# A place of its own for every operation of every batch in the order of a four-layer kernel's engines

## The chip, the cores and the metric

The kernel runs on one core of one Trainium2 chip. A core has TensorE (matrix products, in the profile PE, with its weight loads as PEld), VectorE (DVE), ScalarE (ACT) and GpSimd (POOL), each of which works through its own instructions in order, and SyncE (SP), which issues most transfers. The engines wait for one another by semaphores. The metric is the device time of the slowest core, here the only one, in microseconds (us).

## What is computed

A batch of 8 sequences of 128 rows with 128 channels goes through four layers. Each layer is attention and then a feed-forward network (FFN), each added to the stream with a gate, `x = x + tanh(g) * f(x_norm)`:

```python
# layer 0: 16 heads of 64 over a context, causal mask
attn = softmax(where(causal | padding, NEG, q @ k.T / sqrt(64)))     # ctx @ Wo.T
y = bitlinear(silu(bitlinear(x, w_gate)) * bitlinear(x, w_up), w_down)   # ternary weights, x rounded to 8 bits
# layer 1: 16 heads of 8 with a mask, then 8 experts, the top 2 of each row
buf = zeros.at[dest].set(xr); y = gelu(buf @ W1 + b1) @ W2 + b2; out = sum of y[dest] * gates
# layer 2: one head of 128 with padding by lengths, then a ternary FFN with gelu and a layernorm
# layer 3: 16 heads of 8 with biases, then a ternary FFN with two rmsnorms and a squared relu
```

## The kernel before

One batch fills the 128 partitions, so each stage of a layer is run once for each of the eight batches. The stages are named A0, F0 (layer 0), A1, ROUTE and MOE (layer 1, ROUTE choosing the experts and MOE running them, one expert after the other over all batches), A2, F2, A3, F3. For each engine a table `stages` holds the operations of every stage: for A0 on VectorE for instance `ln_stats` (mean and variance), `v_sb` (copies a half of the values out of a bank), `top_of` (maxima of four heads' scores), `recip0` (inverse sums of the exponentials), `ot_sb0` and `resid`.

Sixteen heads are worked in four groups of four. On TensorE `scores0` makes two groups' scores into two banks (the mask first, added as a product with the identity, line 810), ScalarE's `exps` turns them into probabilities (line 565) with VectorE's maxima, GpSimd's `norm0` multiplies them by the inverse sums (line 468), `probsT` transposes them (line 866), `probsT_sb` copies them back, `pv0` multiplies by the values, `y0` by the output weights. `proj0` makes keys, queries and values (lines 903 and 908), `xt` transposes the normalised rows (line 801), `up`, `ht` and `y_ffn` are the FFN's three products (lines 975, 986, 997). GpSimd's `rs` is the inverse root of a variance and the normalisation behind it (lines 441 to 462), `masks` makes the masks of layers 1 and 2 (lines 427 to 436), `scatter` and `fetch` move single rows to and from the experts by indirect transfers (lines 483 and 488). In A2 VectorE sums the fetched rows of a batch (`sum_stats`, line 1444), takes the maxima of its scores (`top2`, line 1270) and normalises its product (`norm2`, lines 1276 and 1278); in F3 it quantises (`quant3`, `scale3`, `square3`, `hq3`).

The order is set by pattern. `steps_of` lays the stages out in steps, with a start for each stage (`PLAN`: F0 four steps behind A0, A1 six, ROUTE eleven; then the experts; then A2, F2, A3 and F3 in the same way). In each step every stage has four slots, and in a slot each operation works on the batch that its own lag gives it; `turns` lets the stages of one slot take turns, an instruction each. So all batches have the same neighbours, apart from the first and the last ones, where stages are still or already missing. Things that are done once hang on a step's start or end: `masks` behind the second step of A0, `weight_sums` (sums of the ternary weights, which need a bank that the values had) ahead of a step, `banks_free`, `ternary_ready`, `start_inner` (waits only), `first_fetches` (the first two batches' rows) ahead of A2, where `fetch_ahead` then fetches two batches ahead.

A bank of the accumulator memory is claimed before it is written: `claim` finds which operation had it before, by the order on TensorE, and waits for the one that emptied it. So a new order gives new claims.

## Time and profile before

| | |
|---|---|
| time, median of 3 runs (lowest to highest) | 484.13 us (484.13 to 485.12) |
| span of the profiled execution | 482.6 us |
| busy in it: TensorE, its weight loads | 388.5 us (81%), 281.1 us (58%) |
| busy in it: VectorE, ScalarE, GpSimd | 287.2 us (60%), 263.1 us (55%), 180.6 us (37%) |

The profiled execution has a span of its own, 482.6 us, from its first to its last instruction; the measured times are 1.5 us and more above it, for what lies around. The span is read here by stages: A0 and F0 up to some 150, A1 and ROUTE up to some 260, the experts up to 305, A2 and F2 up to some 360, A3 and F3 to the end. A row of the timeline has the start, the duration, the engine, the line and the operation, the tiles, and in brackets how long the engine stood idle before it and which instruction ended that. A row of the table by windows has for each engine the busy time in the stretch and the granted clock of TensorE (PEclk; 1.00 is 2.4 GHz, 0.50 is 1.2 GHz).

### The profile page before, as it was taken

How to read it: one execution, taken by the hardware profiler on the slowest of the kernel's cores; microseconds unless marked ns; L12 is line 12 of the kernel's file. 1: busy time of each engine (PE TensorE's matmuls, PEld its weight loads, DVE VectorE, ACT ScalarE, POOL GpSimd, SP SyncE). 2: the span in 40 equal slices, each digit the busy share in tenths (PEclk: the TensorE clock that was granted, in tenths of full speed). 3: DMA queues.
4: the chain of work that ended last, by engine and by line, in shares of the span. 5: the costliest groups of instructions: out<-in, count | busy, mean ns of one | idle time of the engine just before them, and what ended most of it. 6: DMA issues, size and time to landing. Idle time of an engine off the chain costs nothing.

```text
span 482.6 us, 9945 instructions
## 1 busy us (share of the span) xinstructions
PE 388.5 (81%) x3550; PEld 281.1 (58%) x3564; DVE 287.2 (60%) x859; ACT 263.1 (55%) x781; POOL 180.6 (37%) x294
## 2 busy tenths in 40 slices
PE   3866999999997898999962999427778999889633
PEld 0645777767876665665541899315555666665522
DVE  3151575688687878665562121643546566898884
ACT  3234757676675778877631433422464766555532
POOL 3186334333424311355363000388726442221120
PEclk9597999999999999999985899855699999999955
DMA  8990000000000030000003241111000000000001
GB/s 338 394 381 6 1 2 1 1 2 2 2 1 1 1 133 1 1 13 18 20 22 93 59 130 36 45 33 27 7 0 1 3 1 1 2 2 3 3 0 43
DMA packets 7135, 22.11 MB, mean 46 GB/s; under 512 B 1215, under 2 KB 3503, under 8 KB 6575
## 3 DMA queue, kind: packets, MB, share of 16 engines
q1 hardware_dynamic: 6063, 19.38, 11.1%
q0 software_dynamic: 1024, 2.10, 1.5%
q8 instruction: 29, 0.48, 0.4%
q14 instruction: 19, 0.16, 0.1%
HBM read 14.60 MB, written 6.88 MB: 44 GB/s over the span
## 4 chain that ended last, share of the span: by engine, by line
PE 61%; ACT 11%; POOL 9%; DVE 7%; issue 7%; DMA 3%; SPq 0%; POOLq 0%; another core or an unknown queue 0%; DVEq 0%; ACTq 0%
PE bank L839 6%; PE bank L908 6%; PE bank L866 5%; ACT prob L565 5%; PE bank L1031 4%; PE bank L1022 3%; POOL moe_rows L488 3%; PE bank L822 3%; PE bank L854 3%; PE bank L903 3%; PE bank L917 3%; PE bank L810 3%; DVE mx L1236 3%; PE bank L888 2%; PE bank L975 2%
## 5 line engine op out<-in xcount | busy, mean ns | idle before, releaser
L565 ACT ACTIVATE prob<-bank,mx 128x128 f32<-128x128 f32 x256 | 82.3, 384 | 23.4 <-DVE mx L1236 23.2
L1236 DVE TENSOR_REDUCE mx<-bank 128x4 f32<-128x512 f32 x96 | 63.9, 682 | 41.0 <-PE bank L839 21.5
L468 POOL TENSOR_TENSOR prob<-prob,rden 128x512 f32<-128x512 f32 x32 | 33.2, 1039 | 69.2 <-DVE rden L1258 69.2
L550 ACT ACTIVATE probT<-bank 128x512 f32<-128x512 f32 x64 | 39.5, 617 | 29.9 <-PE bank L866 29.8
L866 PE MATMUL bank<-pack,prob 128*128 128x128 f32 x256 | 41.5, 286 | 7.6 <-POOL prob L468 4.6
L443 POOL TENSOR_TENSOR rstd<-rstd,minus_half 128x1 f32<-128x1 f32 x72 | 41.3, 573 | 6.0
L441 POOL TENSOR_SCALAR rstd<-mv 128x1 f32<-128x1 f32 x64 | 12.4, 193 | 83.0 <-DVE mv L1211 79.6
L866 PEld LDWEIGHTS bank<-pack,prob 128*128 128x128 f32 x256 | 28.7, 143 | 16.4 <-POOL prob L468 6.6
L488 POOL DMA_INDIRECT moe_rows<-yrows_d,row_of x16 | 16.0, 999 | 52.2 <-DMA yrows_d<-o_n 48.3
L462 POOL TENSOR_SCALAR xn<-pack,mv,rstd 128x128 f32<-128x128 f32 x32 | 25.9, 811 | 5.9 <-POOL rstd L443 5.4
L565 ACT ACTIVATION_READ_ACCUMULATOR prob<-bank,mx 128x1 f32 x128 | 27.9, 218 | 0.0
L888 PE MATMUL bank<-probT,vz 128*32 128x128 f32 x512 | 26.9, 282 | 0.6 <-ACT probT L583 0.6
L839 PE MATMUL bank<-kz,qz 64*128 64x512 f32 x96 | 26.4, 626 | 0.5 <-issue 0.5
L583 ACT ACTIVATE probT<-bank 128x512 f32<-128x512 f32 x32 | 18.1, 594 | 14.7 <-PE bank L854 14.6
L891 PE MATMUL bank<-probT,pack 128*32 128x128 f32 x512 | 25.7, 273 | 0.0
L550 ACT ACTIVATE xnT<-bank 128x128 f32<-128x128 f32 x40 | 11.3, 282 | 25.6 <-PE bank L801 25.5
L1247 DVE COPY va<-bank 128x512 f32<-128x512 f32 x16 | 11.0, 688 | 21.4 <-PE bank L903 21.4
L908 PE MATMUL bank<-xnT,pack 128*128 128x128 f32 x128 | 20.6, 311 | 3.1 <-ACT xnT L550 2.9
L810 PE MATMUL bank<-neg,identb 128*128 128x512 bf16 x64 | 20.4, 381 | 3.2 <-ACT prob L565 3.1
L908 PE MATMUL bank<-pack 128*128 128x128 f32 x128 | 18.5, 290 | 4.7 <-DMA pack<-pack_d 2.8
L1435 DVE TENSOR_TENSOR o_n<-bank,pack 90x256 f32<-90x256 f32 (+1 forms) x16 | 4.9, 349 | 28.7 <-PE bank L1031 28.7
L908 PEld LDWEIGHTS bank<-xnT,pack 128*128 128x128 f32 x128 | 18.4, 219 | 6.0 <-ACT xnT L550 4.6
(233 smaller groups left out, 965.2 us busy)
## 6 DMA issues: line engine op xcount, KB each, us to landing
yrows_d<-moe_rows SPq DMA_DIRECT2D x2, 1510.0 KB, 21.2
pack<-pack_d SPq DMA_DIRECT2D x1, 2112.0 KB, 15.7
expert<-experts_d SPq DMA_DIRECT2D x4, 514.0 KB, 8.5
pack<-experts_d SPq DMA_DIRECT2D x4, 514.0 KB, 5.1
pack<-pack_d SPq DMA_DIRECT2D x1, 2048.0 KB, 10.3
xrows_d<-moe_rows SPq DMA_DIRECT2D x1, 1080.0 KB, 21.0
moe_rows<-xrows_d SPq DMA_DIRECT2D x8, 135.0 KB, 3.0
yrows_d<-o_n SPq DMA_DIRECT2D x8, 135.0 KB, 1.8
```

Source lines behind the costliest of these rows:

```text
L443: pool.tensor_tensor(out, out, minus_half, ALU.pow).then_inc(ev.sem, 1)
L462: pool.tensor_scalar(out, x_sb[:, it.b, :], mv[layer][:, k, 0:1], rstd[layer][:, k, 0:1], ALU.subtract, ALU.mult).then_inc(ev.sem, 1)
L468: pool.tensor_tensor(part, part, r.to_broadcast([P, GH, P]), ALU.mult).then_inc(E[A0]["norm"].sem, 1)
L488: pool.indirect_dma_start(y_got[:, b, j, :], None, yrows_d, bass.IndirectOffsetOnAxis(ap=row_of[:, b, j:j + 1], axis=0)).then_inc(y_fetche ...
L550: act.activation(dst, src, ACT.Identity if kw else ACT.Copy, **kw).then_inc(E[layer][name].sem, 1)
L565: act.activation(prob[:, g % 2, P * j:P * j + P], bank[S_BANK[g % 2]][:, P * j:P * j + P], ACT.Exp, bias=mx[:, g % 2, j:j + 1], **kw).then ...
L810: pe.matmul(bank[S_BANK[g % 2]][:, :].rearrange("p (h t) -> p h t", h=GH), identb[:, :], (neg0 if layer == A0 else neg1)[:, bass.ds(it.b, ...
L839: pe.matmul(bank[S_BANK[a]][:, :].rearrange("p (h t) -> p h t", h=GH), qz[rows, it.k, c, :], kt[c if layer == A3 else 0][rows, it.b, :, :] ...
L866: mm_ = pe.transpose(bank[T_BANK[g % 2]][:, P * j:P * j + P], prob[:, g % 2, P * j:P * j + P], ident)
L888: pe.matmul(out[QW * j:QW * j + QW, 0:P], vz[:, it.k, QW * h:QW * h + QW], probT[:, g, P * j:P * j + P], start=(g == 0), stop=(g == G - 1) ...
L908: mm_ = pe.matmul(out[:, P * t:P * t + P].rearrange("p (a n) -> p a n", a=1), w[:, 512 * c + P * t:512 * c + P * t + P], rhs, start=True, ...
L1236: dve.tensor_reduce(out, bank[S_BANK[g % 2]][:, :].rearrange("p (h t) -> p h t", h=GH), AX.X, ALU.max, negate=True).then_inc(E[layer]["max ...
```

## The change

`walk` no longer goes through steps. Every entry of `stages` has eight numbers, a place for each batch, and each engine does its operations in the order of these numbers. An operation of several instructions (a generator) goes back into the queue after each of them with its place raised by `TURN`, so that two such operations can alternate. The things done once have a place too. `steps_of`, `turns`, `LAG` and `PLAN` are gone; the waits that hung on a step's start are now at the operation that needs them, and VectorE has some waits that the fixed pattern had made unnecessary. The instructions of each engine are the same ones.

```diff
+def walk(stages, once=(), run=lambda layer, fn, it, *args: fn(it, *args)):
+    queue = []
+    for layer, entries in stages.items():
+        for b in range(B):
+            for fn, *args, places in entries:
+                if places[b] is not None:
+                    queue.append((places[b], len(queue), run, (layer, fn, Item(b, b), *args)))
+    for at, fn in once:
+        queue.append((at, len(queue), fn, ()))
+    while queue:
+        at, n, begin, args = head = min(queue, key=lambda entry: entry[0:2])
+        queue.remove(head)
+        rest = begin(*args)
+        if rest is not None:
+            if next(rest, stages) is not stages:
+                queue.append((at + TURN, n, lambda rest=rest: rest, ()))
...
-PLAN = (steps_of({F0: 4, A0: 0, A1: 6, ROUTE: 11})
-        + [("steps", [(MOE, s)]) for s in range(NE + 2)]
-        + steps_of({A2: 0, F2: 3, A3: 8, F3: 13}))
+TURN = 0.203
...
+        E[A0]["mean"] = Event(wsum_dve, 0, len(TERNARY))
+        emptied[A0, "w"] = ("mean", 1)
...
-                    [(3, rs, A2), (2, fetch_ahead)],
+                    (fetch_ahead, (322.8, 334.816, 338.348, 287.3, 310.874, 347.278, 324.985, 338.972)),
+                    (rs, A2, (308.589, 313.824, 338.456, 339.08, 343.782, 344.785, 351.472, 352.962))],
...
+            walk(stages, [(-7.2, masks), (279.7, first_fetches)])
...
                 found = before_in_bank(layer, piece, it.rep)
                 if found is None:
+                    if bank_of(layer, piece, it.rep) in K4_BANK[0]:
+                        pe.wait_ge(k4_act, 4)
+                        pe.wait_ge(k4_dve, 4)
                     return
...
             def up(it, layer, piece, w, lhs):
                 wait(pe, layer, "xt_sb", it)
+                if it.rep == 0 and layer == F0:
+                    pe.wait_ge(tern_dve, 9)
+                if it.rep == 0 and layer == F2:
+                    pe.wait_ge(k4_act, 12)
+                    pe.wait_ge(k4_dve, 12)
...
-            def weight_sums():
+            def weight_sums(it):
                 pe.wait_ge(wsum_dve, len(TERNARY))
-                wait(pe, A0, "v_sb", Item(2, 2))
+                claim(it, A0, "w")
                 pe.matmul(bank[R_BANK[0]][:, 0:len(TERNARY)], ones, asum[:, :], start=True, stop=True).then_inc(wsum_pe, 1)
-                pe.wait_ge(wsum_dve, len(TERNARY) + 1)
...
+                wait(dve, layer, "rs", it.back(2))
```

Three places in the order follow, before and after.

The first is VectorE at the start, from the copies of batch 0's last four pieces of keys (`kz`) on. `BN_STATS` and `BN_AGGR` are a batch's statistics, `va` the values, `mx` the maxima of the scores. Before:

```order
L1532 TENSOR_SCALAR kz<-bank,pack 128x4x128 x4
L1210 BN_STATS stats<-pack 128x6
L1211 BN_AGGR mv<-stats 128x2
L1247 COPY va<-bank 128x512 x2
L1210 BN_STATS stats<-pack 128x6
L1211 BN_AGGR mv<-stats 128x2
L1236 TENSOR_REDUCE mx<-bank 128x4 x2
```

After:

```order
L1508 TENSOR_SCALAR kz<-bank,pack 128x4x128 x4
L1183 BN_STATS stats<-pack 128x6
L1184 BN_AGGR mv<-stats 128x2
L1220 COPY va<-bank 128x512
L1183 BN_STATS stats<-pack 128x6
L1184 BN_AGGR mv<-stats 128x2
L1220 COPY va<-bank 128x512
L1209 TENSOR_REDUCE mx<-bank 128x4 x2
```

The statistics of batch 1 stand between the two copies instead of behind both.

The second is TensorE from the last maxima of layer 0 to the first of layer 1: `neg,identb` with `k,qT` is half of a batch's scores, here of batch 7, `prob` the transposes, `probT,va` the product with the values, `oT` the output, `hid` and `t_downT` the FFN. Before:

```order
L810 MATMUL bank<-neg,identb 128x512 x2
L822 MATMUL bank<-k,qT 128x128 x8
L866 MATMUL bank<-pack,prob 128x128 x4
L876 MATMUL bank<-probT,va 64x128 x8
L810 MATMUL bank<-neg,identb 128x512 x2
L822 MATMUL bank<-k,qT 128x128 x8
L866 MATMUL bank<-pack,prob 128x128 x4
```

After:

```order
L754 MATMUL bank<-neg,identb 128x512 x2
L766 MATMUL bank<-k,qT 128x128 x8
L820 MATMUL bank<-probT,va 64x128 x8
L810 MATMUL bank<-pack,prob 128x128 x8
L861 MATMUL bank<-pack,oT 128x128 x8
L939 MATMUL bank<-pack,hid 128x128 x4
L950 MATMUL bank<-t_downT,hqT 128x128 x4
L754 MATMUL bank<-neg,identb 128x512 x2
L766 MATMUL bank<-k,qT 128x128 x8
```

Between the two halves of the scores stand four more of the transposes, an output product and the two products of an FFN.

The third is where A2 begins, on GpSimd (`moe_rows` is a gather, two for each batch; the three rows behind it an inverse root and its normalisation), and on VectorE (`moe_rows` the sums, two for each batch, `mx` the maximum, `rden` and `o_n` the normalisation). GpSimd before:

```order
L488 DMA moe_rows<-yrows_d,row_of 128x128 x6
L441 TENSOR_SCALAR rstd<-mv 128x1
L443 TENSOR_TENSOR rstd<-rstd,minus_half 128x1
L462 TENSOR_SCALAR pack<-pack,mv,rstd 128x128
L488 DMA moe_rows<-yrows_d,row_of 128x128 x2
L441 TENSOR_SCALAR rstd<-mv 128x1
L443 TENSOR_TENSOR rstd<-rstd,minus_half 128x1
L462 TENSOR_SCALAR pack<-pack,mv,rstd 128x128
L488 DMA moe_rows<-yrows_d,row_of 128x128 x2
```

After:

```order
L438 DMA moe_rows<-yrows_d,row_of 128x128 x6
L391 TENSOR_SCALAR rstd<-mv 128x1
L393 TENSOR_TENSOR rstd<-rstd,minus_half 128x1
L412 TENSOR_SCALAR pack<-pack,mv,rstd 128x128
L438 DMA moe_rows<-yrows_d,row_of 128x128 x2
L391 TENSOR_SCALAR rstd<-mv 128x1
L393 TENSOR_TENSOR rstd<-rstd,minus_half 128x1
L412 TENSOR_SCALAR pack<-pack,mv,rstd 128x128
L438 DMA moe_rows<-yrows_d,row_of 128x128 x6
```

By the table the first six gathers are those of batches 0, 1 and 2 before and of 0, 1 and 5 after, and the last six of after are those of 2, 3 and 4. VectorE before, from the second batch's sums on:

```order
L1444 SCALAR_TENSOR_TENSOR pack<-moe_rows,w_tok,pack 128x128 x2
L1210 BN_STATS stats<-pack 128x6
L1211 BN_AGGR mv<-stats 128x2
L1270 TENSOR_REDUCE mx<-bank 128x1
L1444 SCALAR_TENSOR_TENSOR pack<-moe_rows,w_tok,pack 128x128 x2
L1210 BN_STATS stats<-pack 128x6
L1211 BN_AGGR mv<-stats 128x2
L1270 TENSOR_REDUCE mx<-bank 128x1
L1276 RECIPROCAL rden<-rden 128x1
```

After:

```order
L1243 TENSOR_REDUCE mx<-bank 128x1
L1420 SCALAR_TENSOR_TENSOR pack<-moe_rows,w_tok,pack 128x128 x2
L1183 BN_STATS stats<-pack 128x6
L1184 BN_AGGR mv<-stats 128x2
L1420 SCALAR_TENSOR_TENSOR pack<-moe_rows,w_tok,pack 128x128 x2
L1183 BN_STATS stats<-pack 128x6
L1184 BN_AGGR mv<-stats 128x2
L1249 RECIPROCAL rden<-rden 128x1
L1251 TENSOR_SCALAR o_n<-bank,rden 128x128
L1243 TENSOR_REDUCE mx<-bank 128x1
```

Behind the first batch's maximum stand the sums of two batches, 2 and 3, instead of one, and then batch 0's normalisation ahead of batch 1's maximum.

## Rows read from the trace of the kernel before

**Rows 1.** The page's first lines: span, and busy time of each engine.

```profile
span 482.6 us, 9945 instructions
...
PE 388.5 (81%) x3550; PEld 281.1 (58%) x3564; DVE 287.2 (60%) x859; ACT 263.1 (55%) x781; POOL 180.6 (37%) x294
```

**Rows 2.** Windows: stretch and length, each engine's busy time, PEclk, DMA.

```profile
41.00:138.00 97.00, 91.59 (x809) 71.75 (x811) 65.06 (x183) 65.06 (x254) 36.26 (x49) 0.98 0.01 2
138.00:160.00 22.00, 18.80 (x178) 15.01 (x179) 16.04 (x46) 15.51 (x62) 8.74 (x11) 1.00 0.01 1
160.00:248.00 88.00, 82.01 (x922) 52.05 (x922) 61.62 (x192) 65.41 (x209) 34.49 (x58) 1.00 0.08 26
...
305.00:346.00 41.00, 21.74 (x82) 13.40 (x80) 21.13 (x73) 14.00 (x39) 30.94 (x46) 0.58 0.11 29
346.00:367.00 21.00, 15.05 (x83) 10.78 (x83) 10.62 (x37) 13.38 (x29) 9.94 (x21) 0.92 0.00 1
367.00:447.00 80.00, 74.91 (x908) 51.07 (x914) 60.57 (x173) 48.10 (x97) 25.70 (x57) 1.00 0.01 2
```

**Rows 3.** Timeline of VectorE at the start: start, duration, operation, idle before.

```profile
24.53 0.69 DVE L1247 COPY va<-bank 128x512 f32<-128x512 f32 x1 [2.08 <-PE bank L903]
```

**Rows 4.** Timeline of GpSimd at the start.

```profile
25.72 0.19 POOL L441 TENSOR_SCALAR rstd<-mv 128x1 f32<-128x1 f32 x1 [11.06 <-DVE mv L1211]
...
32.23 6.21 POOL L436 TENSOR_SCALAR neg<-pack,lens_f,qneg 128x128 bf16<-128x128 f32 x8
38.41 2.03 POOL L468 TENSOR_TENSOR prob<-prob,rden 128x512 f32<-128x512 f32 x2
```

**Rows 5.** Timeline of TensorE at the start.

```profile
19.81 1.92 PE L903 MATMUL bank<-pack 128*128 128x512 f32 x2
...
39.49 1.11 PE L866 MATMUL bank<-pack,prob 128*128 128x128 f32 x4 [4.37 <-POOL prob L468]
```

**Rows 6.** Windows: the stretch of the low clock near 40.

```profile
37.40:44.20 6.80, 4.71 (x18) 3.98 (x19) 0.18 (x1) 3.48 (x14) 4.08 (x5) 0.50 0.00 0
```

**Rows 7.** Timeline of SyncE's queue: issue of the large mask's load.

```profile
3.90 0.45 SPq L379 DMA_DIRECT2D mask_i<-mask_d  x1
```

**Rows 8.** The tile of that mask: time from issue to landing.

```profile
DMA to landing us min/median/max: 16.4/16.4/16.4
```

**Rows 9.** Timeline of TensorE at the last scores of layer 0.

```profile
149.56 0.39 PE L810 MATMUL bank<-neg,identb 128*128 128x512 bf16 x1 [0.71 <-ACT prob L565]
151.44 0.39 PE L810 MATMUL bank<-neg,identb 128*128 128x512 bf16 x1 [1.50 <-ACT prob L565]
```

**Rows 10.** Timeline of GpSimd behind the experts: first gather, first root, next gather.

```profile
307.87 0.99 POOL L488 DMA_INDIRECT moe_rows<-yrows_d,row_of  x1 [48.29 <-DMA yrows_d<-o_n]
...
315.29 0.19 POOL L441 TENSOR_SCALAR rstd<-mv 128x1 f32<-128x1 f32 x1
...
317.22 1.08 POOL L488 DMA_INDIRECT moe_rows<-yrows_d,row_of  x1 [0.18 <-issue]
```

**Rows 11.** Timeline of VectorE there: batch 1's maximum.

```profile
323.13 0.29 DVE L1270 TENSOR_REDUCE mx<-bank 128x1 f32<-128x128 f32 x1 [2.78 <-PE bank L957]
```

**Rows 12.** Transfers issued from 305 to 335: count, median us to landing.

```profile
moe_rows<-yrows_d,row_of POOLq DMA_INDIRECT x15, 2.5
```

**Rows 13.** Timeline of TensorE: second down projection of F2, first scores of A3.

```profile
359.60 0.49 PE L994 MATMUL bank<-crow,pack 128*128 128x128 f32 x2 [1.74 <-ACT hid L550]
...
367.44 1.13 PE L839 MATMUL bank<-kz,qz 64*128 64x512 f32 x4 [0.48 <-issue]
```

**Rows 14.** Timeline of TensorE at the tail: batch 7's output product.

```profile
462.05 0.79 PE L942 MATMUL bank<-pack 128*128 128x128 f32 x2 [5.09 <-DVE pack L1226]
```

**Rows 15.** Timeline of VectorE at the tail: batch 7's normalisation, batch 3's last residual.

```profile
457.81 0.94 DVE L1263 RECIPROCAL rsum<-bank 128x128 f32<-128x128 f32 x1
...
458.78 0.29 DVE L1265 TENSOR_TENSOR oT<-bank,rsum 128x128 f32<-128x128 f32 x1
...
461.66 0.34 DVE L1226 SCALAR_TENSOR_TENSOR pack<-bank,hs,pack 128x128 f32<-128x128 f32 x1
```

426 lines of the change are left out of this document (205 added, 221 removed).

## The prediction

> **What bounds the kernel now.** Read first the busy shares: TensorE is busy 388.5 of 482.6 us, VectorE 287.2, ScalarE 263.1 [rows 1]. An average hides where time can be won, so next the table by stage [rows 2]. In the three attention stretches with sixteen heads TensorE stands still little: 97.00 - 91.59 = 5.4 us in 41 to 138, 88.00 - 82.01 = 6.0 in 160 to 248, 80.00 - 74.91 = 5.1 in 367 to 447. The larger holes are between: about half of 305 to 346 is idle and the granted clock there is 0.58 of full, 346 to 367 has 6.0 us idle, 138 to 160 has 3.2 us. A new order can win only at these seams, at the start, at the tail, or by closing the 16.5 us of small gaps in the dense stretches.
>
> The change keeps every operation and its tile; it only gives each a new neighbour on its engine, and moves some waits from a step's head to the operation that needs them. So no instruction is added or taken away, and each term below is a wait that goes, shrinks or appears. I followed each engine's new order by hand through the rows' times.
>
> **The start: minus 4.0 us.** On VectorE the statistics of batch 1 stand behind both copies of batch 0's values. The second copy starts at 24.53, after a wait of 2.08 us for TensorE, and takes 0.69 [rows 3]; the statistics follow it. GpSimd, which waits 11.06 us for them, then does batch 1's inverse root at 25.72, the twelve mask instructions up to 32.23 + 6.21 = 38.4, and only then the first normalisation, at 38.41 [rows 4]. TensorE's first transposes of probabilities wait 4.37 us for that [rows 5]. While it waits its clock falls: 37.4 to 44.2 has 4.71 us of matmul at 0.50 [rows 6].
>
> In the new order TensorE does batch 0's first values ahead of its first queries, and VectorE takes batch 1's statistics between the two copies. The values, 1.92 us from 19.81 on [rows 5], then start in the queries' place, behind the transposed rows near 17.6; they need only the context, which is there, and the copy is at about 19.6 to 20.3, the statistics end near 20.9, and GpSimd's row of 25.72 moves to about 21.0. The large mask was asked for at 3.90 us [rows 7] and took 16.4 us to land [rows 8], so it was there at 20.3 and holds nothing up. It is then through its masks at 33.7 and the first normalisation moves by 4.7 us. TensorE has more to do before that point (the second values of batch 1 are put ahead of the transposes), so its wait nearly goes, and with it the low clock: 4.71 us at half speed are 2.35 at full. The ceiling is therefore 4.37 + 2.35 = 6.7, the floor 0 if TensorE were the later one all the same. Following the rows on, the last of batch 0's four transposes comes 3.9 us earlier and the scores of batch 2 stay ahead by 3.75. I take 4.0, near the normalisation's own 4.7, less a little for the new order's extra work ahead.
>
> **First to second attention: minus 1.5 us.** At 149.56 and 151.44 TensorE waits 0.71 and 1.50 us, because the last scores of batch 7 need banks that ScalarE's exponentials must empty, and those wait for a maximum that stands behind the gated FFN's quantisation on VectorE [rows 9]. The new order puts batch 6's first product with the values, two transposes, batch 5's output and batch 3's down projection between the two halves of the scores, some 5 us of ready work. Bounds 0 and 2.2; I take 1.5, since the work drawn forward leaves small holes behind it.
>
> The Trainium skill (Perfetto Trace Analysis, Optimization Strategy) says that a kernel whose most contended engine changes over time may gain by interleaving those regimes. By that rule all the idle time of 138 to 160, 22.00 - 18.80 = 3.2 us, could go, and the sum below would be -7.7 and the time 476.4. The rows show only 2.2 us of it at the place that the new order touches, so I stay with 1.5.
>
> **The gathers of the third attention: plus 0.5 us, bounds -2 and +6.8.** Here the new order looks worse. After the experts GpSimd gathers two sets of rows for each batch; three batches take 315.29 - 307.87 = 7.42 us, 2.47 each, and an inverse root holds the next gather up by 317.22 - 315.29 = 1.93 [rows 10]. Before, it gathers 0, 1 and 2, and then alternates one inverse root and one gather. After, it gathers 0, 1, 5, then 6, and only then 2, 3 and 4, all three in a row. And VectorE now has the sums of batches 2 and 3 ahead of batch 0's normalisation and batch 1's maximum. So that maximum, which comes at 323.13 [rows 11], must wait for batch 3's rows: GpSimd reaches the gather of 3 at 307.87 + 5 x 2.47 + 2 x 1.93 = 324.1, ends it at 326.5, the rows land 2.5 us after their issue [rows 12], about 1.5 after its end, and two sums, the statistics and the normalisation take 1.9 us. That is 329.9, or +6.8. Batch 0's residual comes 4.6 us later by the same reckoning.
>
> What catches it: batches 2 to 4 then come close together, where before each pair of gather and root, 2.47 + 1.93 = 4.4 us, set their distance, and the third FFN's second transpose now stands ahead of the first down projection, so that TensorE's wait of 1.74 us at 359.60 shrinks [rows 13]. By hand the first up projection comes 4 us later, the second down projection 1.5 us later than 359.60, and the scores of the fourth attention at 367.44 are at -1 to +0.5 [rows 13]. I take +0.5. The upper bound is open to one more thing, the clock: TensorE has 15.05 us of matmul in 346 to 367 at 0.92 [rows 2], and if it stayed at 0.50 there, these would take 0.92 / 0.50 - 1 = 0.84 times as long again, 12.6 us, part of it in idle gaps. The forecast counts nothing for it; the second rival does.
>
> **The tail: minus 1.0 us.** Batch 7's output product waits 5.09 us, to 462.05 [rows 14]. Its normalised rows are ready at 458.78 + 0.29 = 459.07, but its bank is emptied by batch 3's last residual, at 461.66, behind 2.6 us of quantisation on VectorE [rows 15]. The new order puts that residual ahead of the normalisation. The output could come 462.05 - 459.07 = 3.0 us earlier; behind it VectorE has a full row of quantisations that are as many as before. Bounds 0 and 3.0; I take 1.0. Route and experts: no seam moves by more than 0.3 us, nothing.
>
> **The dense stretches: 0, bounds -2 and +2.** Each pass of a batch is set by the loop scores, maximum, exponential, transposes, and its members are all still there. Some exponentials now stand back to back, which saves a wait; a few outputs now follow their last product at once, with the normalisation between them exposed (from 457.81 to 459.07 it takes 1.26 us [rows 15]; one or two such places are the 2 us of either bound). These cancel as far as I can follow them. The weight sum of the ternary layers has a place of its own, and the mean on VectorE follows it there without TensorE waiting for it: nothing.
>
> **Sum.** -4.0 - 1.5 + 0 + 0.5 - 1.0 = -6.0 us on the profiled execution's span, 482.6 to 476.6. The median of 484.13 lies 1.5 us above that span, and nothing at either end of the program changes, so 478.1 is the time.
>
> **Rivals.** (1) *No change.* The third attention's 6.8 us pass on in full and cancel the -6.5 of the other terms: 484.4. For it: TensorE is idle for half of that stage, and behind a late batch 1 there is not much other work. Against: the chain there is one of several, and batches 2 to 4 catch up.
>
> (2) *Slower.* The same one mechanism, the gathers of 5 and 6 ahead of 2 and 3, with the clock: TensorE, idle longer, stays at half clock up to the fourth attention. To the 6.8 us come 0.84 x 15.05 = 12.6, of which I let a third be felt where the matmuls stand in the chain, 4.2: -6.5 + 6.8 + 4.2 = +4.5, 488.6. It decides as soon as the first up projection comes over 5 us late and the stretch 346 to 367 shows a clock under 0.7. For it: the clock was 0.58 over 305 to 346 [rows 2], and it comes back only when TensorE works more closely. Against: the FFN's matmuls come closer together in the new order.
>
> (3) *Much faster.* The dense stretches tighten too. They hold 5.4 + 6.0 + 5.1 = 16.5 us of TensorE's idle time; half of it and the forecast's 6.0 give 469.9, all but a sixth of it 464. For it: with a place for each operation an order can fit each batch, where one pattern before served all eight. Against: my walk along the rows found no place where many of these gaps go; ScalarE and VectorE are each busy 65.06 of the 97.00 us [rows 2] and stand in the same loop. The Trainium skill (Perfetto Trace Analysis, Identifying the Most-Contended Engine) says that matmul busy time is a bad measure of how near the roofline is, and weight-load busy time a better one; weight loads fill 71.75 of 97.00 us in 41 to 138 [rows 2], 74%, so by it more than the idle time could go.
>
> (4) *It does not do what it says:* an operation stands behind a wait that a later one on another engine must release, or a claim of a bank is late everywhere, and the kernel slows by tens of us. I see no such place.
>
> **Chances.** Forecast (475.5 to 482) 0.42; no change 0.13; slower 0.19; much faster 0.24; the rest 0.02, slower. The range leaves out a tenth on each side: from the middle of the much faster case, 468.5, to the slower case's price, 489. About 0.2%, 1 us, is what a measurement of this kernel can tell from no change. Of the no-change case 0.11 lies within that and 0.01 on either side. Faster by more: 0.42 + 0.24 + 0.01 = 0.67; same 0.11; slower 0.19 + 0.02 + 0.01 = 0.22.
>
> **What would show it.** Start: GpSimd's first normalisation near 33.7 instead of 38.4, and no stretch at half clock around 40. First to second attention: under 1 us of waits for exponentials around 146 to 150. Third attention: batch 1's maximum 6 us later against the end of the experts, the fourth attention's first scores within 1 us of before, both counted from the end of the experts. Tail: no 5 us wait for the bank of the output. The forecast is wrong if the dense stretches change length by over 2 us each, or if the third attention's delay reaches the fourth.

## The result

The changed kernel takes 509.09 us (median of 4 runs, 508.50 to 509.18) against 484.13 us (483.57 to 485.12), a ratio of 1.0512 with an interval of 1.0492 to 1.0532. It is slower by 25.0 us where the forecast was 6.0 us faster, and 20.1 us above the upper end of the range.

The first lines of the page of after, to be read beside [rows 1]:

```profile
span 507.3 us, 10007 instructions
PE 387.7 (76%) x3550; PEld 279.3 (55%) x3564; DVE 287.6 (57%) x859; ACT 261.6 (52%) x781; POOL 182.3 (36%) x294
```

The counts by engine are those of before and the busy times lie within 2 us of it (the 62 instructions more are none that count as busy); the span is 24.7 us longer. So nothing costs more: all of the loss is time in which engines stand still.

Where it lies is told by the windows of after, cut about where the program's places answer to the windows of [rows 2], with the start (13 to 41 before) ahead of them (stretch and length, busy time of TensorE, weight loads, VectorE, ScalarE, GpSimd, granted clock, DMA):

```profile
13.00:40.00 27.00, 22.73 (x124) 15.88 (x124) 6.73 (x16) 9.01 (x33) 16.50 (x23) 0.94 0.87 333
35.00:145.00 110.00, 93.32 (x830) 72.97 (x833) 66.22 (x184) 65.40 (x255) 39.71 (x52) 1.00 0.02 7
145.00:172.00 27.00, 20.78 (x195) 15.77 (x195) 17.91 (x55) 16.18 (x65) 9.33 (x14) 1.00 0.01 1
172.00:269.00 97.00, 78.28 (x842) 48.96 (x846) 60.96 (x184) 63.61 (x204) 32.72 (x55) 1.00 0.07 24
388.00:474.00 86.00, 75.57 (x935) 53.36 (x938) 61.91 (x176) 46.57 (x93) 25.48 (x56) 0.98 0.01 2
```

The second to the fourth line are layers 0 and 1. TensorE is busy 93.32 + 20.78 + 78.28 = 192.4 us in them, and in [rows 2] 91.59 + 18.80 + 82.01 = 192.4: nearly the same work (1867 products for 1909, since the windows do not cut at the same ones). But it is idle 41.6 us of 234 there, where it was idle 14.6 us of 207. The granted clock is 1.00, so no clock explains it. The last line, layer 3, has 10.4 us idle for 5.1.

One length says the same in one number, and can be read off every run: from the start of the first product with the values of batch 0 to the start of the last product with the routing's weights. It is 205.6 us before and 233.6 us after, 28.0 more. The start ahead of it is 3.4 us shorter (46.05 for 49.47), and what follows it up to the end of TensorE's last product (224.1 us before, 224.3 after) is as long as it was. I call this length the **front**, and what follows it the **back**. The windows that cut there, before and then after:

```profile
49.47:255.05 205.58, 187.22 (x1864) 134.76 (x1872) 143.99 (x430) 140.68 (x504) 81.61 (x120) 0.99 0.04 13
46.05:279.61 233.56, 190.09 (x1865) 134.99 (x1872) 145.54 (x432) 140.94 (x502) 80.54 (x117) 0.99 0.03 12
```

With the same products but one, TensorE is idle 18.4 us before and 43.5 after: 25.1 of the 28.0 us are idle time.

These lengths come from one execution of each kernel, and the start is not the same in every one: in the five traces whose start has the order of before (before, e1, e3, e5, e6), the first product with the values is at 48.3 to 50.5; in the four with that of after (after, e2, e4, e11) it is at 45.5 to 46.2. A difference of 1 or 2 us between the starts of two traces can be chance.

What TensorE waits for there, totals of the waits by line in 35 to 269 of after (us in total, times, longest):

```profile
PE bank L754 <- ACT prob L498: 11.5, 14, 2.0
PE bank L870 <- ACT xnT L483: 3.0, 3, 1.2
PE bank L847 <- DVE va L1220: 2.1, 1, 2.1
PE bank L810 <- ACT prob L498: 2.0, 3, 0.9
```

The same view of before, 41 to 248:

```profile
PE bank L810 <- ACT prob L565: 3.1, 5, 1.5
PE bank L801 <- ACT k L550: 2.3, 6, 0.4
PE bank L908 <- ACT xnT L550: 2.2, 6, 0.4
```

Before, TensorE has many waits of 0.4 us. After, one line leads: the mask ahead of a batch's scores (`mask_scores`, L754) waits 14 times, up to 2.0 us, for a bank that ScalarE's exponentials (`exps`, L498) have to empty; 13 times it is the second of the two banks. It is 8.4 us more than the same line had before (L810, 3.1 us), so it is not the whole loss. Summed over all lines of the two views, the waits grow from 13.4 to 40.3 us: those that ScalarE ends from 10.8 to 30.7, those that VectorE ends from 2.1 to 7.4, GpSimd's from 0.2 to 1.7. The rest of ScalarE's share is copies, one or a few times each.

One of these waits, first on TensorE of after (start, duration, line, operation, idle before and what ended it):

```profile
99.88 1.06 PE L852 MATMUL bank<-pack 128*128 128x128 f32 x8
100.78 0.38 PE L754 MATMUL bank<-neg,identb 128*128 128x512 bf16 x1
102.98 0.39 PE L754 MATMUL bank<-neg,identb 128*128 128x512 bf16 x1 [1.83 <-ACT prob L498]
```

And on ScalarE of after:

```profile
99.05 0.37 ACT L498 ACTIVATE prob<-bank,mx 128x128 f32<-128x128 f32 x1 [2.27 <-DVE mx L1209]
...
100.44 1.09 ACT L483 ACTIVATE probT<-bank 128x512 f32<-128x512 f32 x2
101.39 0.40 ACT L498 ACTIVATE prob<-bank,mx 128x128 f32<-128x128 f32 x1
...
102.42 0.42 ACT L498 ACTIVATE prob<-bank,mx 128x128 f32<-128x128 f32 x1
102.76 0.65 ACT L483 ACTIVATE k<-bank 128x512 f32<-128x512 f32 x1
```

ScalarE does two groups of four exponentials, about 1.4 us each, with two copies of transposed probabilities between them. The second group ends at 102.84, and TensorE, which has the mask of the first bank done and wants the second, stands from 101.15 to 102.98. The keys that TensorE made at 99.88 are copied behind all that, from 102.76. The first group had itself waited 2.27 us for VectorE's maxima.

The same pass before, on TensorE:

```profile
97.74 1.09 PE L876 MATMUL bank<-probT,va 128*64 128x128 f32 x16
99.22 0.30 PE L801 MATMUL bank<-pack,xn 128*128 128x128 f32 x1 [0.39 <-ACT k L550]
99.89 1.16 PE L908 MATMUL bank<-xnT,pack 128*128 128x128 f32 x8 [0.37 <-ACT xnT L550]
100.89 1.02 PE L903 MATMUL bank<-pack 128*128 128x512 f32 x2
101.75 0.59 PE L810 MATMUL bank<-neg,identb 128*128 128x512 bf16 x2
```

And on ScalarE:

```profile
98.13 0.38 ACT L565 ACTIVATE prob<-bank,mx 128x128 f32<-128x128 f32 x1
...
98.47 0.61 ACT L550 ACTIVATE k<-bank 128x512 f32<-128x512 f32 x1
98.95 0.62 ACT L550 ACTIVATE probT<-bank 128x512 f32<-128x512 f32 x1
99.56 0.28 ACT L550 ACTIVATE xnT<-bank 128x128 f32<-128x128 f32 x1
99.74 0.36 ACT L565 ACTIVATE prob<-bank,mx 128x128 f32<-128x128 f32 x1
```

Here too three copies stand between the two groups. But each is one that TensorE needs at once: it is released twice after 0.4 us (99.22, 99.89), and with products, a transpose, queries and values to do, it comes to the mask only when both groups are through, so the mask has no wait at all.

### The profile page after: what moved, and what is told of

The parts are those of the page before. It is cut to its first block and busy times, and to the rows that moved or that the text cites. A ratio compares the mean times of both kernels' runs of the same rounds, so it can differ in the third digit from the quotient of the medians.

```text
span 507.3 us, 10007 instructions
## 1 busy us (share of the span) xinstructions
PE 387.7 (76%) x3550; PEld 279.3 (55%) x3564; DVE 287.6 (57%) x859; ACT 261.6 (52%) x781; POOL 182.3 (36%) x294
## 3 DMA queue, kind: packets, MB, share of 16 engines
q1 hardware_dynamic: 6063, 19.38, 10.4%
## 5 line engine op out<-in xcount | busy, mean ns | idle before, releaser
L498 ACT ACTIVATE prob<-bank,mx 128x128 f32<-128x128 f32 x256 | 81.7, 387 | 17.7 <-DVE mx L1209 13.3
L483 ACT ACTIVATE probT<-bank 128x512 f32<-128x512 f32 x64 | 37.9, 610 | 25.2 <-PE bank L810 25.0
L810 PE MATMUL bank<-pack,prob 128*128 128x128 f32 x256 | 39.0, 280 | 7.8 <-ACT prob L498 2.0
L810 PEld LDWEIGHTS bank<-pack,prob 128*128 128x128 f32 x256 | 28.1, 141 | 16.6 <-issue 6.9
L754 PE MATMUL bank<-neg,identb 128*128 128x512 bf16 x64 | 22.3, 394 | 11.7 <-ACT prob L498 11.5
L498 ACT ACTIVATION_READ_ACCUMULATOR prob<-bank,mx 128x1 f32 x128 | 29.0, 226 | 0.0
L783 PE MATMUL bank<-kz,qz 64*128 64x512 f32 x96 | 27.7, 653 | 1.0 <-ACT qz L483 0.8
L516 ACT ACTIVATE probT<-bank 128x512 f32<-128x512 f32 x32 | 18.5, 596 | 13.0 <-PE bank L798 12.9
L433 POOL DMA_INDIRECT xrows_d<-xn_all,row_of x16 | 16.5, 1029 | 23.4 <-DVE row_of L1383 20.8
L847 PE MATMUL bank<-pack 128*128 128x512 f32 x32 | 19.9, 707 | 5.1 <-DVE va L1220 2.1
L483 ACT ACTIVATE k<-bank 128x512 f32<-128x512 f32 x16 | 9.8, 612 | 22.4 <-PE bank L852 22.4
## 6 DMA issues: line engine op xcount, KB each, us to landing
pack<-pack_d SPq DMA_DIRECT2D x1, 2048.0 KB, 10.4
```

The lines of the kernel that those rows point to most:

```text
L483: act.activation(dst, src, ACT.Identity if kw else ACT.Copy, **kw).then_inc(E[layer][name].sem, 1)
L498: act.activation(prob[:, g % 2, P * j:P * j + P], bank[S_BANK[g % 2]][:, P * j:P * j + P], ACT.Exp, bias=mx[:, g % 2, j:j + 1], **kw).then ...
L754: pe.matmul(bank[S_BANK[g % 2]][:, :].rearrange("p (h t) -> p h t", h=GH), identb[:, :], (neg0 if layer == A0 else neg1)[:, bass.ds(it.b, ...
L783: pe.matmul(bank[S_BANK[a]][:, :].rearrange("p (h t) -> p h t", h=GH), qz[rows, it.k, c, :], kt[c if layer == A3 else 0][rows, it.b, :, :] ...
L810: mm_ = pe.transpose(bank[T_BANK[g % 2]][:, P * j:P * j + P], prob[:, g % 2, P * j:P * j + P], ident)
L847: mm_ = pe.matmul(out[:, :], ctxT[:, it.b, :], col["wvT_0"][:, 512 * c:512 * c + 512], start=True, stop=True)
```

## The experiments

Four theories were put to the test. **P** (theory A in the expectations of e1 to e3): some places of the table are bad in the front, and it is the order there, not the new waits. **A1** (not the stage of that name): ScalarE's places keep a ready operation waiting. **S**: ScalarE's groups of exponentials stand ahead of copies that TensorE needs next. **T**: TensorE's own order leaves too little between an operation and the one that needs its result, and no order of the other engines mends that; V in the expectations is the contrary. Other letters are explained in the expectation that uses them.

The runs in one table: the measured median and that of before measured beside it, the ratio with its interval, and the lengths of front and back from the trace, which is one execution.

| run | us | before | ratio | front, back |
|---|---|---|---|---|
| before | | 484.13 | | 205.6, 224.1 |
| after | 509.09 | 484.13 | 1.0512 [1.0492, 1.0532] | 233.6, 224.3 |
| e1_front_pattern | 483.24 | 485.25 | 0.9973 [0.9947, 1.0000] | 205.2, 222.9 |
| e2_back_pattern | 509.74 | 485.25 | 1.0512 [1.0459, 1.0565] | 234.9, 224.7 |
| e3_all_pattern | 485.34 | 485.25 | 1.0006 [0.9988, 1.0024] | 205.2, 224.0 |
| e4_start_only | 482.25 | 485.0 | 0.9945 [0.9927, 0.9963] | 206.3, 224.6 |
| e5_third_only | 481.08 | 485.0 | 0.9922 [0.9891, 0.9953] | 205.2, 221.4 |
| e6_tail_only | 481.64 | 485.0 | 0.9938 [0.9910, 0.9967] | 205.2, 222.9 |
| e7_act_by_ready | 510.7 | 485.0 | 1.0530 [1.0502, 1.0559] | 238.3, 223.8 |
| e8_after_short_exp | 491.51 | 484.29 | 1.0134 [1.0107, 1.0161] | 216.1, 223.9 |
| e9_before_short_exp | 476.32 | 484.29 | 0.9824 [0.9797, 0.9850] | 198.6, 223.9 |
| e10_copies_first | 507.72 | 484.29 | 1.0473 [1.0446, 1.0501] | 229.8, 223.0 |
| e11_three_edges | 476.48 | 484.29 | 0.9830 [0.9804, 0.9856] | 206.6, 218.9 |
| e12_after_by_ready | 516.46 | 485.2 | 1.0645 [1.0621, 1.0669] | 242.2, 224.3 |
| e13_before_by_ready | 511.31 | 485.2 | 1.0565 [1.0524, 1.0606] | 232.0, 224.2 |
| e14_after_act_need | 500.43 | 484.42 | 1.0345 [1.0303, 1.0388] | 225.2, 222.0 |
| e15_before_act_need | 494.24 | 484.42 | 1.0196 [1.0166, 1.0226] | 215.9, 224.0 |
| e16_before_act_ready | 501.36 | 484.42 | 1.0335 [1.0295, 1.0374] | 223.4, 223.5 |

### Which half, and order or waits: e1, e2, e3

The old walk by steps stands beside the new one, and each engine takes one or the other for the front half (layers 0 and 1 and the experts) and the back half; the waits are those of after in all three. In these lines the letters S and T are not the theories: S is the pattern by steps, T the tables.

```diff
+BY = {'pe': 'ST', 'act': 'ST', 'dve': 'ST', 'pool': 'ST'}    # e1_front_pattern
+BY = {'pe': 'TS', 'act': 'TS', 'dve': 'TS', 'pool': 'TS'}    # e2_back_pattern
+BY = {'pe': 'SS', 'act': 'SS', 'dve': 'SS', 'pool': 'SS'}    # e3_all_pattern
...
+        if BY[name][half] == "S":
+            walk_steps(None, plans[half], {n: old[n] for n in old if n in halves[half]}, before, after, run)
+        else:
+            walk({n: stages[n] for n in stages if n in halves[half]}, [(at, fn) for h, at, fn in once if h == half], run)
```

> The changed kernel, but up to the end of the experts every engine has the order of the kernel before; from the third attention on the tables stay. Theory A (the tables of the first two layers cost the time: TensorE stands idle there 24 us more, the stages behind them are worth nothing either way, +24.4 us at the third attention's first product and +24.7 at the end): 484 to 485 us. Theory B (the new waits, which this kernel keeps, cost a good part): 490 to 505. Theory C (the loss of the second half is only hidden because the first half is late): 488 or more.

> The other way round: tables up to the end of the experts, the order of the kernel before from the third attention on. Theory A: 508 to 510 us. Theory C: 503 or less. By the trace the third attention gains 3 to 6 us by its table and the fourth gives them back, so that this kernel should have the third attention later and the fourth shorter than the changed kernel, with the same end.

> The order of the kernel before on every engine and for all stages, with the waits of the changed kernel where it has them (at the first use of a bank, at the operation that needs a weight, and the extra ones on VectorE). Theory A: 484.1 us within 1. Theory B: 490 to 505, since only the waits differ from the kernel before.

With the old order in the front the kernel is at 483.24, with the old order in the back at 509.74. So the loss is all in the order of the first two layers and the experts. The back's order is worth 2 us at most: e1 is 2.1 us below e3, at the edge of what the intervals tell apart, and e2 and after have the same ratio. With the old order everywhere and the new waits kept it is at 485.34, a ratio of 1.0006 [0.9988, 1.0024]: the waits that were moved cost nothing that shows. P stands, for the half; which engine's places, these runs don't say.

### The prediction's three terms, each alone: e4, e5, e6

The old order, written as positions, with the order of after in one place only: the first 44.5 us, the third attention up to the first scores of the fourth, the last 33 us. Of each a line or two:

```diff
-                    (rs, A0, (0, 1, 7, 12, 17, 23, 29, 35)),
+                    (rs, A0, (0, 1, 5, 8, 17, 23, 29, 35)),            # e4_start_only
-                    (proj0, 'v', 0, (4, 12, 26, 43, 59, 78, 99, 120)),
+                    (proj0, 'v', 0, (3, 11, 26, 43, 59, 78, 99, 120)), # e4_start_only
-                    (fetch_ahead, (74, 76, 78, 80, 82, 84, 99999, 99999)),
+                    (fetch_ahead, (78, 79, 80, 74, 76, 85, 99999, 99999)), # e5_third_only
-                    (resid, A3, (592, 616, 643, 672, 701, 728, 750, 771))],
+                    (resid, A3, (592, 616, 643, 672, 701, 734, 743, 771))], # e6_tail_only
```

> The order of the kernel before on every engine, but for the operations that the changed kernel begins in its first 44.5 us: those stand in front in the changed kernel's order. The forecast's term of the start alone. Theory A (the start's 4 us are real, and it is the later passes' order that spends them): the scores of batch 2 come some 4 us earlier than before and the lead stays to the end, 480 to 481.5 us. Rival D (the lead is lost to whatever comes next, in any order): 484 to 485.

> The order of the kernel before, but for the third attention and what the changed kernel begins up to the fourth attention's first scores: those stand in the changed kernel's order, the gathers of batches 5 and 6 ahead of 2 and 3 among them. Theory E (the delay of batch 1's maximum is more than made good by the batches that follow closely): the fourth attention's first scores 3 us or more earlier than before, 480 to 482 us. Rival (the delay passes on, as the slower case of the forecast had it): 486 or more.

> The order of the kernel before, but for what the changed kernel begins in its last 33 us, which stands behind the rest in the changed kernel's order: the forecast's term of the tail alone. By the traces the changed kernel's last 33 us win 1 to 3 us against the kernel before: 481.5 to 483.5 us. Rival (the residual ahead of the normalisation only moves VectorE's work): 484 to 486.

All three are faster, by 2.8, 3.9 and 3.4 us against before measured beside them, and by 2.0, 2.0 and 1.0 us of span in the one execution traced. e5 and e6 came out as expected; e4 lies between the 481.5 of its theory and the 484 of the rival.

The start gives about what was worked out and keeps most of it: against the trace of before TensorE is 3.3 us ahead at the first product with the values and 4.07 us at the last scores of layer 0. There it meets the two waits of [rows 9] unchanged, and it loses 1.5 us on the way into layer 1; 2.0 us are left at the end. TensorE of e4:

```profile
145.49 0.39 PE L754 MATMUL bank<-neg,identb 128*128 128x512 bf16 x1 [0.71 <-ACT prob L498]
147.37 0.39 PE L754 MATMUL bank<-neg,identb 128*128 128x512 bf16 x1 [1.50 <-ACT prob L498]
```

In the third attention batch 1's maximum is as late as worked out, but the first scores of the fourth attention come earlier. VectorE, then TensorE, of e5 (the first gather starts at 308.69, 0.82 later than in [rows 10]):

```profile
330.50 0.28 DVE L1243 TENSOR_REDUCE mx<-bank 128x1 f32<-128x128 f32 x1
```

```profile
363.78 1.13 PE L783 MATMUL bank<-kz,qz 64*128 64x512 f32 x4
```

Against [rows 11] the maximum is 7.4 us later, 6.5 counted from the gathers; against [rows 13] the scores are 3.7 us earlier, 4.5 counted so. At the tail of e6 the wait for the bank is gone, and a shorter one for the normalised rows is in its place:

```profile
461.69 0.80 PE L895 MATMUL bank<-pack,oT 128*128 128x128 f32 x2 [3.08 <-DVE oT L1238]
```

### ScalarE by readiness, and exponentials made short: e7, e8, e9, e10

In e7 each operation of ScalarE up to the routing has the moment as its place at which its inputs were there in the trace of after; in e10 the same, with the groups of exponentials put back by up to 1.2 us. A line of each, of batch 0 to 7:

```diff
-                    (exps, A0, 2, (39.34, 57.487, 70.625, 86.716, 108.646, 127.366, 135.779, 151.197)),
-                    (probsT_sb, A0, 1, (39.706, 54.248, 74.486, 93.26, 107.316, 123.836, 139.751, 153.799)),
+                    (exps, A0, 2, (-22.405, -9.17, 9.256, 28.1, 47.9, 67.552, 86.327, 102.984)),           # e7_act_by_ready
+                    (exps, A0, 2, (-21.873, -7.97, 10.456, 28.483, 49.1, 68.752, 86.362, 103.673)),        # e10_copies_first
+                    (probsT_sb, A0, 1, (-21.075, -8.733, 14.986, 28.615, 48.337, 68.551, 90.452, 103.849)), # e7 and e10
```

In e8 (after) and e9 (before) the four exponentials of a group are one instruction. These two kernels leave out the maxima of a group's other three heads in the exponent and the sums of their exponentials:

```diff
             def exps(it, layer, g):
...
+                if it.rep >= 1 or layer == A1:
+                    kw = dict(accum_out=den0[:, g % 2, 0:1]) if layer == A0 else {}
+                    act.activation(prob[:, g % 2, :], bank[S_BANK[g % 2]][:, :], ACT.Exp,
+                                   bias=mx[:, g % 2, 0:1], **kw).then_inc(E[layer]["probs"].sem, GH)
+                    return
```

> The changed kernel, but ScalarE's places up to the end of the routing are new: its operations stand in the order in which, in the changed kernel's trace, their inputs were ready. All other engines stay as changed. Theory A1 (ScalarE's own order, which keeps copies waiting behind operations that are not ready or long, makes TensorE wait): a third or more of the 24 us comes back, 492 to 501 us. Rival A2 (the places of TensorE and VectorE are as much to blame, and ScalarE only passes on their lateness): 505 to 510.

> The changed kernel with shorter exponentials in the first two attentions: from the second batch on (in the second attention from the first) each group of four heads is one ScalarE instruction over 512 columns with the first head's maximum, instead of four over 128 columns, so that ScalarE holds its queue 0.6 us where it held it 1.4; the other heads' maxima are left out of the exponent and their sums are not taken. All orders stay. Theory S (what TensorE waits for in the changed kernel is mostly a copy or an exponential that stands ready while ScalarE is at another one, 22 of 38 us by the trace, against 6 of 15 before): 12 us or more come back, 497 us or less, and the distance to the kernel before with the same shorter exponentials falls from 25 to 15 us or less. Rival O (the order is to blame by what it makes wait for what, ScalarE's time is not): both kernels gain alike and the distance stays above 20.

> The kernel before with the same shorter exponentials (the same parts left out). Theory S: it has little to gain, 0 to 6 us, 478 to 485 us. Rival O: as much as the changed kernel.

> The changed kernel, but ScalarE's places up to the end of the routing are new: by the time at which the inputs were ready in the changed kernel's trace, as in the experiment before, but exponentials of the first two attentions are put back by up to 1.2 us, never past the point at which they began, so that a copy that comes within that time goes first. Theory S: better than by readiness alone (510.7), 500 to 508 us, since a copy that TensorE waits for no longer stands behind a whole group of exponentials that came just before it; not near 484, since the exponentials themselves are waited for too. Rival O: 509 to 513.

e7 felled A1 as far as readiness goes. Worked out from the semaphores in the traces, over the 224 operations that ScalarE has up to the routing, the mean time from inputs ready to start is 0.54 us before, 0.96 after and 0.55 in e7: e7 nearly halves the wait of after and yet stays at 510.7. A mean says nothing on which operation waits. The pattern of before lets the gate's tanh wait (0.94 us) and layer 0's exponentials (0.92), and the small copies that TensorE needs next hardly at all: 0.07 us for the FFN's rounded rows (`xq_sb`), 0.15 for layer 1's transposed rows (`xt_sb`), 0.18 for layer 0's queries. In e7 the gate waits 0.05 and the exponentials 0.74, but these copies 1.15, 0.80 and 0.74; in after they waited 1.06, 0.79 and 0.60.

That led to S. The one instruction takes 0.69 us where the four took 1.4. ScalarE of e9:

```profile
95.19 0.69 ACT L565 ACTIVATE prob<-bank,mx 128x512 f32<-128x512 f32 x1 [1.70 <-DVE mx L1241]
```

With it after gains 17.6 us and before 8.0, so the distance falls from 24.8 to 15.2 us. Some 10 us of the loss therefore hang on how long a group of exponentials takes. S is half right: before gained more than the 0 to 6 us of S, so it too waits for the exponentials. And the two runs don't tell a group that keeps other work from ScalarE from a group whose own result comes too late: the shorter one helps both. e10, the cheap cure by S, is at 507.72, inside S's 500 to 508 at its very edge; that is 3 us better than e7 and 1 to 2 us better than after, no more.

### The same rule on both kernels: e12, e13, e16, and e14, e15

In e12 (after) and e13 (before) TensorE keeps its order, and ScalarE, VectorE and GpSimd each do their operations in the order in which the inputs were there in that kernel's trace. In e16 (before) only ScalarE does so: e7 is its counterpart. In e14 (after) and e15 (before) ScalarE goes by the latest start at which nothing in that kernel's trace would come later. A line or two of each, in positions (the lines that go are the orders of before and, last, of after, in the same form):

```diff
-                    (xt_sb, A0, (2, 8, 21, 34, 47, 62, 78, 94)),
-                    (exps, A0, 2, (12, 25, 38, 52, 68, 84, 100, 113)),
-                    (probsT_sb, A0, 1, (14, 27, 40, 54, 70, 86, 102, 114)),
+                    (xt_sb, A0, (2, 9, 22, 35, 48, 63, 79, 95)),            # e13, e16
+                    (exps, A0, 2, (12, 25, 38, 52, 67, 83, 99, 112)),       # e13, e16
+                    (probsT_sb, A0, 1, (14, 27, 40, 55, 71, 87, 103, 115)), # e13, e16
+                    (xt_sb, A0, (2, 7, 18, 31, 44, 59, 75, 91)),            # e15
+                    (exps, A0, 2, (11, 25, 37, 52, 68, 84, 100, 113)),      # e15
...
-                    (probsT_sb, A0, 1, (13, 26, 41, 54, 69, 84, 103, 114)),
+                    (probsT_sb, A0, 1, (14, 25, 41, 52, 68, 84, 103, 114)), # e12
+                    (probsT_sb, A0, 1, (14, 29, 42, 53, 71, 87, 101, 115)), # e14
```

> The changed kernel with TensorE's order as it is, but up to the end of the routing ScalarE, VectorE and GpSimd take their operations in the order in which the inputs were ready in the changed kernel's trace (operations of one kind keep their order among themselves, and VectorE's operations of several instructions stand by their beginning). Theory T (TensorE's order sets when work comes to the other engines, in bunches, and no order of theirs mends that): 503 to 512 us. Theory V (VectorE's or GpSimd's own order costs what ScalarE's did not): 498 us or less.

> The same with the kernel before: its TensorE order, and up to the end of the routing the three other engines by the readiness in its own trace. Theory T: the order of the other engines matters little while TensorE's stays, 483 to 488 us, so that this kernel and the one above, which have the same rule for three engines, differ by 18 us or more. Theory V: 490 us or more, since the pattern of the other engines was what made it good.

> The changed kernel, but up to the end of the routing ScalarE takes its operations in the order of the latest moment at which each could begin without anything in the changed kernel's trace coming later (by need, not by readiness). Theory V (the table's ScalarE order does not fit what TensorE needs next): 8 us or more come back, 501 us or less. Theory T (TensorE's order is at fault, whatever ScalarE does): 505 to 512.

> The kernel before with the same rule for ScalarE, by need in its own trace: the control for the rule. If an order by need is a good one, 482 to 487 us; if it is 495 or more, the rule itself is bad and the experiment with the changed kernel says nothing of theory T.

> The kernel before with ScalarE by readiness in its own trace, the other engines as they were. With all three helpers by readiness it took 511.3 us. If ScalarE's order is what cost that (copies behind exponentials that were ready a little earlier): 500 us or more. If VectorE's or GpSimd's: 490 or less.

e13 is the run that settled most, against T: with TensorE's good order untouched, the helpers' order alone costs 26 us, as much as the whole change. And e16 shows that ScalarE alone brings 17 of these. Yet in e16 no operation of ScalarE is moved by more than two positions; 104 of the 224 are moved. The waits of TensorE in e16, 35 to 270:

```profile
PE bank L745 <- ACT k L483: 7.3, 6, 2.1
PE bank L852 <- ACT xnT L483: 5.4, 6, 1.2
```

In before the same two waits were 2.3 and 2.2 us, also six times each. The copy of a batch's second half of the keys stood behind the rest of a group of exponentials before too, 0.65 us in most batches; now more of the group is ahead of it, and it waits 0.99 to 2.36 us. That of the transposed rows never waited and now waits 0.77 us in five batches. The mean wait on ScalarE is 0.42 us in e16, lower than before. ScalarE and then TensorE of e16, where the keys were ready at 105.60:

```profile
105.23 0.36 ACT L498 ACTIVATE prob<-bank,mx 128x128 f32<-128x128 f32 x1
...
106.60 0.61 ACT L483 ACTIVATE k<-bank 128x512 f32<-128x512 f32 x1
```

```profile
107.36 0.30 PE L745 MATMUL bank<-pack,xn 128*128 128x128 f32 x1 [0.74 <-ACT k L483]
```

In e13 the two waits are as long (7.2 and 5.4 us), and one that GpSimd ends comes on top, for the normalised probabilities (`norm0`):

```profile
PE bank L810 <- POOL prob L418: 9.8, 8, 2.1
```

What they stand behind, on GpSimd or on VectorE, was not followed.

With ScalarE by the same rule the two kernels stand at 510.7 and 501.36 (readiness, by ratios 1.0530 and 1.0335) and at 500.43 and 494.24 (need): 6 to 9 us apart, not 25. (The runs of e14 lie 495.34 to 502.76, so its distance is the less certain.) With all three helpers by readiness they are 5.2 us apart (e12, e13) where T asked for 18 or more; e12 itself, at 516.46, is slower than either theory had it, so the rule makes after worse as well. e14 is the one order tried for after that helps clearly, by 8 to 9 us; its waits, 35 to 260, show the leading line shorter and spread:

```profile
PE bank L754 <- ACT prob L498: 6.8, 11, 0.9
PE bank L810 <- POOL prob L418: 4.0, 6, 1.8
```

e15 warns of reading too much into it: the rule itself costs before 9.8 us, and its 494.24 lies just under the 495 from which, by its expectation, e14 says nothing of T.

**What is shown and what stays open.** Shown: the loss is order, not waits (e3); it is in the front (e1, e2); an order of the three helpers alone can cost as much (e13), and one of ScalarE alone two thirds of it (e16); with one rule for ScalarE in both kernels, 16 to 19 of the 25 us between them go. That ScalarE's table carries that much of the change is likely and not shown: the rules slow before by 10 to 26 us, and may cover what the other tables cost. By the front's length of the traces the rest is larger, 9 to 15 of 28 us. Open: how the loss is shared among the tables of the four engines. A kernel with one engine's table from after and the others from before would tell; it wasn't run.

### The three edges together: e11

> The order of the kernel before, with the changed kernel's order in three places at once: its first 44.5 us, the third attention up to the fourth attention's first scores, and the last 33 us. By the traces of the three apart they win 2.4, 2.2 and 1.2 us. Theory A (the edges are independent): 5 to 8 us less than the kernel before, 477 to 479 us where the latter has 484 to 485. Rival D: less than 3 us.

The edits are those of e4, e5 and e6 in one kernel. It takes 476.48 us, 0.9830 [0.9804, 0.9856] of before, and beats both kernels. The start is 3.7 us shorter, the front 1.0 longer, the back 5.2 shorter: together the 7.8 us of its span's gain (474.8 for 482.6). By the medians it gains 7.8 us too, within the 5 to 8 of its theory and less than the 10.0 that the three have in sum. What the third attention does for it shows in the window from the experts' end to the fourth attention's first scores, which lasts 62.8 us before. Before, then e11:

```profile
304.60:367.40 62.80, 37.19 (x165) 24.34 (x164) 32.36 (x110) 27.77 (x68) 41.20 (x67) 0.70 0.07 19
302.00:359.50 57.50, 32.52 (x156) 21.76 (x155) 32.31 (x108) 27.40 (x68) 40.43 (x65) 0.73 0.08 21
```

The stretch is 5.3 us shorter, with 9 of 165 products put behind it and the clock at 0.73 for 0.70. TensorE's idle time in it hardly changes, 25.0 us for 25.6.

## Why the prediction was wrong

**The dense stretches, "0, bounds -2 and +2", are the step that failed.** The front, which holds two of the three and the seam between them, became 28.0 us longer, and the third, layer 3, some 5 us. "Its members are all still there" was true and beside the point: the loop of scores, maximum, exponential and transposes was kept, but what stands between its members on ScalarE wasn't followed: of the 26.9 us that TensorE's waits grew by in the dense part, ScalarE ends 19.9. How far its own table is to blame stays open, as said above. "Some exponentials now stand back to back, which saves a wait" is neither borne out nor the fault: up to the routing two groups stand next to each other at 1 place of ScalarE's order before and at 12 in after, but also at 15 in e14, which is faster than after, and at 4 in e7, which is not. The walk along the rows covered the start, three seams and the tail, and no pass in the middle, where the pattern repeats and where all of the loss is. A term that repeats in every pass can't be bounded by "one or two such places": the one wait at L754 alone came 14 times and to 11.5 us, for 5 times and 3.1 us before. In layer 3 it is VectorE that TensorE waits for: the view of 387.1 to 483.6 of after, and that of 367.4 to 456.1 of before:

```profile
PE bank L789 <- DVE mx L1209: 5.3, 5, 2.4
```

```profile
PE bank L845 <- DVE mx L1236: 1.8, 3, 0.8
```

**The start, -4.0, was right in mechanism and measured 3.4.** The second half of batch 0's values no longer holds the statistics up. VectorE and GpSimd of after:

```profile
21.04 0.69 DVE L1220 COPY va<-bank 128x512 f32<-128x512 f32 x1 [8.23 <-PE bank L847]
21.65 0.28 DVE L1183 BATCH_NORM_STATS2 stats<-pack 128x6 f32<-128x128 f32 x1
```

```profile
28.74 6.21 POOL L386 TENSOR_SCALAR neg<-pack,lens_f,qneg 128x128 bf16<-128x128 f32 x8
34.92 1.03 POOL L418 TENSOR_TENSOR prob<-prob,rden 128x512 f32<-128x512 f32 x1
```

The first normalisation is at 34.92, 3.5 earlier than in [rows 4] and 1.2 later than worked out, since the copy came at 21.04 and not at 20. TensorE's wait of 4.37 [rows 5] is gone, with waits of 1.66 us (31.77) and 1.98 (42.72) in its place, and the clock over the start is 0.94 where it was 0.75 before:

```profile
13.00:41.00 28.00, 18.75 (x105) 13.94 (x104) 7.55 (x15) 7.77 (x26) 15.62 (x20) 0.75 0.84 321
```

The size is good to about 2 us, by the spread of the start between traces; the means of the five traces and the four above are 3.5 us apart. The gain was there at the first product with the values and was spent by the next passes; e4 keeps most of it.

**First to second attention, -1.5, did not come.** Work was drawn forward between the two halves of batch 7's scores, but the masks still wait: 0.71 us at the first half (153.21) and 1.16 at the second, 1.9 in sum where [rows 9] has 2.2. On TensorE of after:

```profile
160.56 0.39 PE L754 MATMUL bank<-neg,identb 128*128 128x512 bf16 x1 [1.16 <-ACT prob L498]
```

And the operations behind it wait too: the stretch has 27.00 - 20.78 = 6.2 us idle, 3.0 more than in [rows 2]. The Trainium skill (Perfetto Trace Analysis, Optimization Strategy) says that interleaving regimes may help; by it 3.2 us could have gone here, and the measurement went the other way.

**The gathers, +0.5: the delay right, what catches it undersized.** The maximum's delay is 6.5 us for 6.8 (e5). But from the end of the experts the fourth attention's first scores come 4.5 us earlier in e5 and 5.4 earlier in after, outside the bound of -2 and the "within 1 us". The same window of after as shown for before and e11:

```profile
329.70:387.10 57.40, 32.56 (x156) 21.72 (x155) 32.23 (x107) 27.45 (x68) 40.40 (x65) 0.73 0.07 21
```

TensorE's idle time in it is hardly less, 24.8 us for 25.6: the waits for the FFN's hidden rows, 3.7 us in three before (1.74 of them at 359.60), are gone, as the prediction had it, and one of 4.88 us for batch 1's probabilities is new. Its busy time is 4.6 us less, with 9 of 165 products put behind the first scores and the clock at 0.73 for 0.70; how these two share the gain is not shown. The back is 2.7 us shorter in e5. After gives the gain back in layer 3, 388 to 474.

**The tail, -1.0: right in mechanism and about in size.** The wait of 5.09 us for a bank [rows 14] became 3.08 in e6 and 3.09 in after, now for the normalised rows; the back of e6 is 1.2 us shorter.

**The rivals.** The slower one had the right sign and the wrong place: the gathers cost nothing in the end, and behind them, from 370 to 388 of after, the clock was 0.92 as before, not under 0.7. *Much faster* was given 0.24 for a place of its own that fits each batch; the Trainium skill's rule that weight-load time is the better measure of distance to the roofline (Perfetto Trace Analysis, Identifying the Most-Contended Engine) was counted for it. In 35 to 145 of after weight loads fill 72.97 of 110 us, 66% where it was 74%: the rule shows that there is room, and not that a given order will use it. The rest, "the kernel slows by tens of us", named the size and a part of the way (a bank that is late everywhere: 8.4 of the 26.9 us of waits) and had 0.02 because no such place had been seen; none had been looked for in the passes.

The Trainium skill (Perfetto Trace Analysis, Optimization Strategy) says that the same gap repeating on the engine that should be saturated can mean too few buffers. Here the wait at L754 repeats 14 times and is for a bank, but tiles and banks are those of before, where it comes 5 times and to 3.1 us: the gap grew with an order (e1, e3), and the number of banks had not changed.

## What to carry to other kernels

When an order is changed, walk at least one full pass of the dense loop on every engine, since a wait there counts once for each pass, and price the seams only afterwards. On an engine that serves the bottleneck in order, the mean wait of its operations is no guide (0.54 us before, 0.55 in e7, 0.42 in e16, with 484, 511 and 501 us); look for the results that the bottleneck needs next and what stands ahead of them. Neither first come, first served nor the latest possible start was as good here as the fixed pattern. Seams can be ordered alone: the changed order at three edges, with the pattern between them, gave 1.7% where the whole table cost 5.1%.

## What was not expected of the hardware

A helper at two thirds load sets much of the pace. ScalarE is busy 65.06 of 97.00 us [rows 2], and moving operations of its by one or two positions cost 17 us (e16). Halving the exponentials' 1.4 us on an engine that isn't the bottleneck gave before 8.0 us (e9), more than any of the edges alone.
